# Relational graph layer on one core: the table stage's stores and order of work, and the queues of the sum stage, are rearranged

## The chip, the cores and the metric

The kernel runs on one core of a Trainium2 chip. The metric is the device time in microseconds (us) of one execution. Engines in the views: PE is the matrix engine, PEld its weight loads, DVE the vector engine, ACT the scalar engine, POOL the engine that issues the gathers, SP the engine that issues most other transfers. PEclk is the clock granted to PE as a share of its full 2.4 GHz.

## The reference

One layer on a graph of 12,500 nodes with 64 features and 200,000 edges, sorted by destination, each with one of 64 relations and a weight. `W` is made from a basis; then every edge brings its source's normed row, times weight, times its relation's 64×64 matrix, to its destination.

```
h = jnp.maximum(_layernorm(x, axis=-1), 0.0)
W = jnp.einsum('rb,bio->rio', comp, basis)
msg = h[src] * norm
s = segment_sum(msg, etype * N + dst, R * N).reshape(R, N, -1)
y = relu(jnp.einsum('rni,rio->no', s, W) + bias) + relu(h @ res_w.T + res_b)
out = x + (y - mean(y, 0)) * rsqrt(var(y, 0) + BN_EPS) * gamma + beta
```

Destinations crowd at low node numbers (drawn as a square), so a tile of 128 edges at the front of the list falls on very few nodes.

## The kernel before

**Two ways for an edge.** The list is cut into 1563 tiles of 128 edges. The first 528 (`HEAD`) are *heads*: the rows of x are gathered, normed, multiplied by a one-hot matrix of (node, relation) on PE and added up in an SBUF array `sacc`; at six chunk ends (after 215, 304, 373, 431, 482 and 528 heads, `HEAD_ENDS`) `sacc` is multiplied by `W` (32 matmuls, the "relations"), flushed into the accumulator `acc` and cleared. The other 1035 tiles read rows of a table: `z_table`, h times every relation's matrix, 800,000 rows of 64 numbers, 205 MB, which the kernel writes first.

**Table stage.** x lies in SBUF; DVE norms it in steps of 14 node tiles (`LNT`). For each of the 25 chunks of 512 nodes DVE duplicates the rows, PE transposes them (`transposed_x`), ACT takes the high part in bf16 with the relu (`first_part`, L684), DVE the remainder (the "split", L881), ACT casts that (`second_part`, L691). A chunk has four node tiles and each tile eight products (128 nodes by 8 relations × 64), each of three bf16 matmuls into one PSUM bank (L1238). ACT copies the banks into `zst` (L655); from node tile 24 (`DVE_FROM`) DVE takes the odd ones of three tiles in four (L983). There are four banks (`zps`), and seven once the metadata is done (chunk 15). `zst` has `NZS` = 4 buffers of `ZT` = 4 products, 1 MB each; SP stores each when full, 196 transfers with rows of 8 KB a partition. PE's order is written out in `jobs`: with `AHEAD` = 2, transposed x of chunk c, a step of metadata (`meta`), then all products of chunk c−2. DVE's order is: norm steps as due, duplicate, split, a metadata step (`take_meta`), its products of c−2. ACT: first part of c, second part of c−1, products of c−2. Statistics of the head (which base each chunk has, whether all fits) come in one piece with the metadata. Meanwhile POOL gathers the heads' rows of x (L590) and SP stores them by blocks of 8 to `head_rows` as `head_due` says.

**Tile stage.** One list `sums`, the same for PE, DVE and ACT, orders tiles and head items: between tiles 4 and about 800 the head items are dealt out evenly. POOL gathers one tile of table rows per instruction (L618) into a ring of 36 (`NY`); a slot is free when PE has used it. Four tiles are a unit: PE adds its products in PSUM (L1356), DVE adds the window into `acc` (`add_up`, L1088). Units have three banks in turn (`NAP`), and unit u's add comes at the end of unit u+2 (`LAG`). DVE makes the one-hots six tiles (L1105) and four heads (L1112) ahead. For heads, in blocks of eight: DVE's `centre` (L1135, after head 2 of the block before), ACT's squares (L749), DVE's `spread` (L1139, after 4), ACT's root, DVE's `factor` (after 5), ACT's two relus per head into `ab` (L762). PE multiplies head t (L1371) into one of `NHP` = 4 banks and first waits for the add of head t−4; DVE adds it to `sacc` (`add_head`, L1098) `HLAG` = 3 heads later, at a chunk end at once. At a chunk end PE runs the 32 relations (L1380), DVE at once waits for them and flushes (L1161), ACT then clears `sacc` in four instructions (L735), and the next adds wait for those. After the last unit the moments, the batch norm and the output follow.

Of the kernel before, what the change touches and what calls it, by code (L numbers as in the profile page):

```python
# [22 lines left out]
ZT = 4  # L23
NZS = 4
# [4 lines left out]
NAP = 3  # L29
LAG = 2  # L30
TILES_AHEAD, HEADS_AHEAD, HQ = 6, 4, 4
# [15 lines left out]
NHOH = 8  # L47
NHP = 4
HLAG = 3
REL_STEP = 1  # L50

# [27 lines left out]
def rgcn_kernel(nc, x, src, dst, etype, weight, basis, comp, bias, res_w, res_b, gamma, beta, out):  # L79
# [39 lines left out]
    METAS_AT = 4  # L119
    HKEYS_AT, ZROWS_AT = 2, 3  # L120
# [7 lines left out]
    epi_after = [unit_end[done_unit[k]] + (n + 1) * DONE_STEP  # L128
                 for k in range(len(DONE)) for n in range(done_from[k + 1] - done_from[k])]
    moments_at = [min(t + NOH + 1, NZT - 1) for t in epi_after]  # L130
# [55 lines left out]
    with ExitStack() as ctx:  # L186
# [54 lines left out]
        wcopy = zst[:, NZS - 1, :, :].rearrange("p t n -> p (t n)").rearrange("p (r f) -> p r f", f=F)  # L241
# [101 lines left out]
        AHEAD = 2  # L343
        jobs = [("comp",), ("resw",)] + [("w", n) for n in range(F // CLS)]
        for c in range(NCH + AHEAD):
            jobs += [("x", c)] if c < NCH else []
            jobs += [("z", r, t) for t in range((c - AHEAD) * 4, min((c - AHEAD + 1) * 4, NT)) if c >= AHEAD for r in range(NCLS)]
# [65 lines left out]
        def head_due(n):  # L413
            return max(0, min(NHB, int((62 + 3.05 * n - 34) / (1.28 * HB))))
# [213 lines left out]
        def _(e):  # L628
# [64 lines left out]
            def products(c):  # L693

                for n in range(c * BANK // P * NST, min((c + 1) * BANK // P, NT) * NST):
                    t, h = STORES[n]
                    rows = LAST if t == NT - 1 else P
                    if n == NZS - 1:
                        e.wait_ge(s_wd, 16)
# [9 lines left out]
            for kind, n in act_order:  # L709
# [12 lines left out]
            second_part(NCH - 1)  # L722
            products(NCH - 2)
            products(NCH - 1)
# [7 lines left out]
            with e.If(flag >= 1):  # L732
# [12 lines left out]
                for kind, n, *_ in sums:  # L745
# [27 lines left out]
                e.wait_ge(s_rel, NHK)  # L773
# [22 lines left out]
        def _(e):  # L796
# [89 lines left out]
            def stats_of_head():  # L886
# [6 lines left out]
                for k, (a, b) in enumerate(zip(chunk_from, HEAD_ENDS)):  # L893
                    e.tensor_reduce(over[:, k:k + 1], span_h[:, a:b], AX, ALU.max)
                    link(e.tensor_reduce(chunk_f[:, k:k + 1], base_h[:, a:b], AX, ALU.min))
                    link(e.tensor_scalar(base_h[:, a:b], base_h[:, a:b], chunk_f[:, k:k + 1], float(HALF), ALU.subtract, ALU.mult))
                    link(e.tensor_reduce(over[:, NHK + k:NHK + k + 1], base_h[:, a:b], AX, ALU.max))
                    e.tensor_scalar(over[:, k:k + 1], over[:, k:k + 1], float(HEAD_NODES[k] - 1), None, ALU.subtract)
# [294 lines left out]
        def _(e):  # L1193
# [97 lines left out]
            for c in range(NCH + AHEAD):  # L1291
                if c < NCH:
                    transposed_x(c)
# [143 lines left out]
```

## Time and profile before

| | us |
|---|---|
| median of 3 runs | 2539.49 |
| lowest, highest | 2535.84, 2551.64 |
| span of the profiled execution | 2559.4 |
| its table stage | 150 to 984 |
| its tile stage | 1047 to 2536 |

The profiled execution is 20 us longer than the median. The page tells each engine's share over the whole span; since the stages have different limits, the views by window are read after it. A window's row gives the busy time of PE, PEld, DVE, ACT and POOL with the number of instructions, then PEclk, the mean busy share of the DMA engines and their GB/s. A row of waits gives the engine, what it writes and its line, behind the arrow what released it, then us in total, times and the longest. In an order of time each row is start, duration, instruction and in brackets the idle time before it with its releaser. "remote" is a releaser that the profile can't name, "issue" is time in which the engine waited for nothing that shows.

### The profile page before, as it was taken

The page shows a single profiled execution, that of the slowest core. Times are in us where ns is not written, and L with a number is a line of the kernel's source. Part 1 is how long each engine was busy: PE and PEld are TensorE (multiplying, and loading weights), DVE is VectorE, ACT ScalarE, POOL GpSimd, SP SyncE. Part 2 cuts the span into 40 slices and gives each one's busy share as a digit, 9 for nine tenths or more (in the row PEclk, how much of TensorE's full clock was granted, in tenths as well). Part 3 has the DMA queues.
Part 4 walks back from the last instruction along what each step waited for, and adds up shares of the span by engine and source line. Part 5 has one row for each costly group of instructions (what it writes and reads, how often), then busy time and mean ns, then how long its engine had stood idle before and what let it go on. Part 6 is the DMA issues. An engine that isn't in the chain of part 4 may idle for free. (4 is left out here: it accounts for less than half of the span.)

```text
span 2559.4 us, 29252 instructions
## 1 busy us (share of the span) xinstructions
PE 1675.1 (65%) x6522; PEld 817.4 (32%) x6571; DVE 1040.2 (41%) x3394; ACT 1003.6 (39%) x2898; POOL 1474.2 (58%) x1565
## 2 busy tenths in 40 slices
PE   1267677867787767466666677768778787872223
PEld 1222222323233222244444434434434343331112
DVE  0442013335233211255555535636546363632324
ACT  0255543424343332655555526526436252610001
POOL 7265535554465553366666666666666666666664
PEclk9997878878798878555555575575565757575656
DMA  7066667767687765111111111111111111111112
GB/s 141 24 244 264 263 250 275 304 234 285 254 341 300 291 230 198 45 42 40 43 40 40 43 28 41 42 27 39 40 31 39 31 40 31 35 23 41 39 41 63
DMA packets 120893, 308.66 MB, mean 121 GB/s; under 512 B 49361, under 2 KB 49644, under 8 KB 95395
## 3 DMA queue, kind: packets, MB, share of 16 engines
q1 hardware_dynamic: 56622, 233.21, 23.4%
q0 software_dynamic: 49504, 50.79, 10.6%
q10 hardware_dynamic: 14588, 22.76, 3.2%
q8 instruction: 54, 0.88, 0.1%
q14 instruction: 125, 1.02, 0.1%
HBM read 80.28 MB, written 226.35 MB: 120 GB/s over the span
## 5 line engine op out<-in xcount | busy, mean ns | idle before, releaser
L618 POOL DMA_INDIRECT shared<-z_table,idx_all x1019 | 967.3, 949 | 605.8 <-issue 233.6
L590 POOL DMA_INDIRECT acc<-in_x,idx_all x520 | 493.9, 950 | 448.5 <-DMA head_rows<-acc 299.7
L1238 PE MATMUL zps<-wp,res 128*128 128x512 bf16 x1915 | 503.3, 414 | 188.8 <-issue 79.9
L655 ACT ACTIVATE zst<-zps 128x512 f32<-128x512 f32 x480 | 276.9, 599 | 365.3 <-PE zps L1238 223.1
L762 ACT ACTIVATE res<-res,hw 128x64 f32<-128x64 f32 x1056 | 357.5, 426 | 104.2 <-issue 53.8
L1371 PE MATMUL mps<-wp,res 128*128 128x160 f32 (+4 forms) x528 | 271.9, 620 | 158.7 <-issue 84.4
L1238 PEld LDWEIGHTS zps<-wp,res 128*128 128x128 bf16 x1956 | 190.1, 103 | 490.6 <-issue 164.5
L1105 DVE TENSOR_SCALAR shared<-iota,rel_all,wgt_all 128x36 f32<-128x36 f32 (+9 forms) x1035 | 307.9, 326 | 62.0 <-ACT res L729 61.5
L1356 PE MATMUL zps<-shared 128*64 128x36 f32 (+9 forms) x1354 | 208.3, 317 | 146.2 <-issue 72.7
L749 ACT ACTIVATE res<-res,hm 128x64 f32<-128x64 f32 x528 | 176.0, 334 | 224.9 <-issue 132.2
L1356 PEld LDWEIGHTS zps<-shared 128*64 128x64 f32 x1354 | 143.7, 197 | 351.6 <-issue 283.3
L983 DVE COPY zst<-zps 128x512 f32<-128x512 f32 (+1 forms) x172 | 117.6, 690 | 298.1 <-PE zps L1238 171.2
L1112 DVE TENSOR_SCALAR wp<-iota,rel_all,wgt_all 128x160 f32<-128x160 f32 (+4 forms) x528 | 211.8, 402 | 0.1
L1380 PE MATMUL zps<-zst,res 128*64 128x256 f32 x384 | 179.0, 608 | 28.6 <-issue 28.3
L1371 PEld LDWEIGHTS mps<-wp,res 128*128 128x128 f32 x528 | 131.7, 309 | 196.5 <-issue 112.0
L1356 PE MATMUL aps<-shared 128*64 128x36 f32 (+9 forms) x684 | 109.9, 316 | 86.7 <-issue 65.1
L1371 PE MATMUL zps<-wp,res 128*128 128x160 f32 (+4 forms) x264 | 136.8, 621 | 42.4 <-issue 25.2
L1371 PE MATMUL aps<-wp,res 128*128 128x160 f32 (+4 forms) x264 | 137.3, 622 | 40.5 <-issue 34.6
L1098 DVE TENSOR_TENSOR zst<-zst,mps 128x160 f32 (+4 forms) x264 | 95.8, 363 | 139.6 <-remote 67.7
L1356 PEld LDWEIGHTS aps<-shared 128*64 128x64 f32 x684 | 75.5, 196 | 195.1 <-issue 172.2
L735 ACT ACTIVATE zst<-ones 128x2048 f32<-128x2048 f32 x24 | 43.8, 1896 | 197.0 <-remote 197.0
L783 ACT ACTIVATE bmv<-bmv,eps 128x1 f32<-128x1 f32 x1 | 0.3, 294 | 295.5 <-DVE bmv L1175 295.5
(202 smaller groups left out, 1306.9 us busy)
## 6 DMA issues: line engine op xcount, KB each, us to landing
z_table<-zst SPq DMA_DIRECT2D x194, 1024.0 KB
wp<-z_table SPq DMA_DIRECT2D x1792, 0.2 KB
head_rows<-acc SPq DMA_DIRECT2D x66, 256.0 KB
res<-head_rows ACTq DMA_DIRECT2D x64, 256.0 KB
shared<-z_table,idx_all POOLq DMA_INDIRECT x1019
acc<-in_x,idx_all POOLq DMA_INDIRECT x520
wp<-z_table ACTq DMA_DIRECT2D x256, 0.2 KB
zst<-in_x ACTq DMA_DIRECT2D x12, 256.0 KB
```

The lines of the kernel that those rows point to most:

```text
L590: e.indirect_dma_start(out=ring[:, b % NRING, i, :], out_offset=None, in_=x, in_offset=bass.IndirectOffsetOnAxis(ap=idx_first[:, t:t + 1] ...
L618: e.indirect_dma_start(out=ys[:, q % NY, :], out_offset=None, in_=table[:, :], in_offset=bass.IndirectOffsetOnAxis(ap=idx_all[:, col:col + ...
L655: e.activation(to, frm, ACT.Copy).then_inc(s_ez, 1)
L749: last = e.activation(hsq[:, i, :], hs[:, n % 2, i, :], ACT.Square, bias=hm[:, n % 2, 0, i:i + 1], accum_out=hm[:, n % 2, 1, i:i + 1])
L762: last = e.activation(ab[:, t % NABS, a, :], hs[:, n % 2, i, :], ACT.Relu, scale=hw[:, n % 2, 0, i, a:a + 1], bias=hw[:, n % 2, 1, i, a:a ...
L983: e.tensor_copy(zst[0:rows, n % NZS, i, :], bank_of(job)[0:rows, :]).then_inc(s_dz, 1)
L1105: e.tensor_scalar(oh[:, t % NOH, 0:w], iota[:, 0:w], rel_all[:, col:col + 1], wgt_all[:, col:col + 1], ALU.is_equal, ALU.mult).then_inc(s_ ...
L1112: e.tensor_scalar(hoh[:, t % NHOH, 0:w], iota[:, 0:w], rel_all[:, t:t + 1], wgt_all[:, t:t + 1], ALU.is_equal, ALU.mult).then_inc(s_hoh, 1)
L1238: last = e.matmul(to, lhsT=stationary(px, pw), rhs=moving(px, pw), start=(a == 0), stop=(a == 2))
L1356: e.matmul(unit_psum(u)[h:h + F, 0:w], lhsT=rows, rhs=oh[:, t % NOH, 0:w], start=(k < 2), stop=(k >= size - 2)).then_inc(s_agg, 1)
L1371: e.matmul(head_psum(t)[:, 0:w], lhsT=ab[:, t % NABS, :, :].rearrange("p a f -> p (a f)"), rhs=hoh[:, t % NHOH, 0:w], start=True, stop=Tru ...
L1380: last = e.matmul(zps[0:F, NZB - 1, 0:SUM_NODES], lhsT=wf[:, q, :], rhs=by_relation[:, q, :], start=(q == 0), stop=(q == HALF - 1))
```

## The change

The stores: `ZT` 4 → 2 and `NZS` 4 → 8, so 392 transfers of 512 KB with rows of 4 KB; the buffers together keep their size. The order of the table stage: PE now does the eight products of a chunk's first tile, then transposes x of the next chunk, then the products of its other three; ACT likewise puts the first part between products of tile 0 and 1, the second part between 1 and 2; DVE does the split and a metadata step of chunk c ahead of its products of c−1. Statistics of the head are done one chunk at a time in six chunks, the decision on the fast path after them. The tile stage: `NAP` and `LAG` are gone; four units share one bank in turns of two, and their adds come together, six tiles after the group's end; three last units stay alone. One-hots are made ten tiles and six heads ahead (eleven head buffers). Heads have five banks. `centre` comes after head 0 of a block, `factor` after head 6. At a chunk end four "drain" items add the waiting heads, `sacc` is cleared in quarters, each when eight relations are done, and the flush comes eight items later.

```
-ZT = 4
-NZS = 4
+ZT = 2
+NZS = 8
-NAP = 3
-LAG = 2
-TILES_AHEAD, HEADS_AHEAD, HQ = 6, 4, 4
+UG = 4
+ADD_LATE = 6
+TILES_AHEAD, HEADS_AHEAD, HQ = 10, 6, 4
-NHOH = 8
-NHP = 4
+NHOH = 11
+NHP = 5
+FLUSH_LATE = 8
+    added_at = [t + ADD_LATE for t in group_end[:LONE]] + [t + 2 for t in group_end[LONE:]]
-        if b + 1 < NHB and k in (2, 4, 5):
-            head_items.append(({2: "centre", 4: "spread", 5: "factor"}[k], b + 1))
+        if b + 1 < NHB and k in (0, 4, 6):
+            head_items.append(({0: "centre", 4: "spread", 6: "factor"}[k], b + 1))
-            head_items += [("relations", n, r) for r in range(0, HALF, REL_STEP)] + [("flush", n)]
+            head_items += [("drain", n)] * (HLAG + 1)
+            head_items += [("relations", n, r) for r in range(0, HALF, REL_STEP)] + [("clear", n)]
+    for n in reversed(range(NHK)):
+        late = FLUSH_LATE if n + 1 < NHK else 0
+        head_items.insert(head_items.index(("clear", n)) + 1 + late, ("flush", n))
...
-            return max(0, min(NHB, int((62 + 3.05 * n - 34) / (1.28 * HB))))
+            return max(0, min(NHB, int((62 + 3.05 * n / 2 - 34) / (1.28 * HB))))
...
-            return (mps[:, 0, :], mps[:, 1, :], zps[:, 0, :], aps[:, 1, :])[t % NHP]
+            return (mps[:, 0, :], mps[:, 1, :], zps[:, 0, :], aps[:, 1, :], zps[:, 2, :])[t % NHP]
-            return (aps[:, 0, :], zps[:, 1, :], zps[:, 2, :])[u % NAP]
+            if u >= LONE:
+                return (aps[:, 0, :], zps[:, 2, :], zps[:, 1, :])[u - LONE]
+            return (aps[:, 0, u % UG * WIN:(u % UG + 1) * WIN], zps[:, 1, u % UG * WIN:(u % UG + 1) * WIN])[u // UG % 2]
...
-                    first_part(n)
                     c = n - X0
                     if c >= 1:
-                        second_part(c - 1)
-                    if c >= 2:
-                        products(c - 2)
+                        products(tiles_of(c - 1)[0:1])
+                    first_part(n)
+                    if c == 0:
+                        second_part(c)
+                    elif c >= 1:
+                        products(tiles_of(c - 1)[1:2])
+                        second_part(c)
+                        products(tiles_of(c - 1)[2:])
...
-                    elif kind == "flush" and n + 1 < NHK:
-                        e.wait_ge(s_rel, n + 1)
-                        for a in range(0, SUM_NODES * HALF, 2048):
-                            clear(sacc[:, a:a + 2048]).then_inc(s_flush, 1)
+                    elif kind == "clear" and n + 1 < NHK:
+                        for q in range(NSC):
+                            e.wait_ge(s_rel, NSC * n + q + 1)
+                            part = sacc.rearrange("p (n r) -> p n r", r=HALF)[:, :, q * HALF // NSC:(q + 1) * HALF // NSC]
+                            e.activation(part, ones[:, 0:1].unsqueeze(2).broadcast_to([P, SUM_NODES, HALF // NSC]),
+                                         ACT.Copy, scale=0.0).then_inc(s_flush, 1)
...
+                    if STATS_AT <= c < STATS_AT + NHK:
+                        stats_of_chunk(c - STATS_AT)
+                    if c == STATS_AT + NHK:
+                        fast_path_or_not()
+                    if c >= 1:
+                        products(c - 1)
...
-                        if k == size - 1 and u >= LAG:
-                            add_up(u - LAG)
+                        while added[0] < len(units) and added_at[added[0]] == t:
+                            add_up(added[0])
...
-                        while len(heads) > (0 if t + 1 in HEAD_ENDS else HLAG):
+                        while len(heads) > HLAG:
                             add_head(heads.pop(0))
+                    elif kind == "drain" and heads:
+                        add_head(heads.pop(0))
...
-                        if k == 0 and u >= NAP:
-                            e.wait_ge(s_acc, u - NAP + 1 + NCLEAR)
+                        if k == 0 and u % UG == 0 and u >= 2 * UG:
+                            e.wait_ge(s_acc, u - UG + NCLEAR)
+                        if u == len(units) - 1 and k == 0:
+                            e.wait_ge(s_acc, LONE + NCLEAR)
```

## Rows read from the trace of the kernel before

**Rows 1.** The page: span, busy share of each engine, two DMA queues.

```profile
span 2559.4 us, 29252 instructions
PE 1675.1 (65%) x6522; PEld 817.4 (32%) x6571; DVE 1040.2 (41%) x3394; ACT 1003.6 (39%) x2898; POOL 1474.2 (58%) x1565
...
q1 hardware_dynamic: 56622, 233.21, 23.4%
...
q10 hardware_dynamic: 14588, 22.76, 3.2%
```

**Rows 2.** Windows: from:to length, busy of PE PEld DVE ACT POOL, clock, DMA, GB/s.

```profile
150.00:984.00 834.00, 613.49 (x2462) 244.63 (x2510) 245.47 (x444) 351.63 (x613) 425.77 (x449) 0.84 0.73 281
741.00:762.00 21.00, 20.47 (x95) 9.23 (x96) 8.94 (x15) 11.09 (x21) 11.38 (x13) 1.00 0.93 367
600.00:622.00 22.00, 9.85 (x32) 3.64 (x33) 12.41 (x48) 7.47 (x13) 9.48 (x11) 0.69 0.43 155
1073.30:1464.50 391.20, 264.83 (x963) 169.61 (x963) 225.61 (x939) 223.83 (x883) 246.38 (x260) 0.50 0.19 41
1464.50:1500.70 36.20, 31.69 (x127) 13.88 (x127) 9.72 (x43) 5.19 (x16) 23.30 (x26) 0.82 0.15 30
2167.50:2259.40 91.90, 70.97 (x202) 33.53 (x200) 55.20 (x191) 49.08 (x169) 58.22 (x61) 0.55 0.15 32
```

**Rows 3.** The gathers of L618: two windows of that line, one in order.

```profile
990.00:2530.00 1540.00, 966.48 (x1019) 0.58 0.17 37
2252.00:2530.00 278.00, 179.05 (x191) 0.60 0.17 35
...
1502.85 0.94 POOL L618 DMA_INDIRECT shared<-z_table,idx_all  x1 [0.30 <-issue]
```

**Rows 4.** Waits from 1047 to 2291, heads' adds, spread and `ab`.

```profile
DVE zst L1098 <- remote: 129.2, 48, 5.6
DVE zst L1098 <- PE mps L1371: 88.9, 58, 3.9
PEld mps L1371 <- ACT res L762: 65.0, 32, 23.1
DVE hm L1139 <- ACT res L749: 46.6, 17, 15.9
```

**Rows 5.** Chunk ends: idle before L1161, a clear, who waited for L735.

```profile
  remote: 67.5, 6
...
1510.01 7.31 ACT L735 ACTIVATE zst<-ones 128x2048 f32<-128x2048 f32 x4 [40.32 <-remote]
...
  DVE zst L1098: 16.3, 4
```

**Rows 6.** Waits from 2291 to 2530, the tail without heads.

```profile
DVE acc L1088 <- remote: 147.7, 27, 11.7
PEld zps L1356 <- DVE acc L1088: 51.4, 8, 11.6
```

**Rows 7.** Table stage in order of time, then its waits from 150 to 984.

```profile
133.72 0.63 ACT L691 ACTIVATE res<-shared 64x512 bf16<-64x512 f32 x1
...
140.54 0.60 ACT L684 ACTIVATE res<-zps 128x512 bf16<-128x512 f32 x1 [1.76 <-PE zps L1195]
...
141.82 0.60 ACT L655 ACTIVATE zst<-zps 128x512 f32<-128x512 f32 x1
...
392.32 1.46 PE L1238 MATMUL zps<-wp,res 128*128 128x512 bf16 x3 [3.01 <-DVE res L881]
...
393.24 1.07 DVE L970 CAST idx_all<-mps 128x520 int32<-128x520 f32 x1
...
PEld zps L1238 <- DVE res L881: 18.7, 8, 4.6
...
PE zps L1238 <- DVE res L881: 14.3, 6, 3.7
```

**Rows 8.** DMA issues from 0 to 1000: KB each, us to landing.

```profile
w_full<-zst SPq DMA_DIRECT2D x1, 1024.0 KB, 3.9
```

More of the change, by code:

```diff
@@ L119, in rgcn_kernel @@
     METAS_AT = 4
+    STATS_AT = METAS_AT + len(METAS) + 1
+    assert METAS[-1] == "zstats" and STATS_AT + NHK < NCH
     HKEYS_AT, ZROWS_AT = 2, 3
@@ L342, in rgcn_kernel, with tiles_of @@
         s_cols, s_low = sem("s_cols"), sem("s_low")
[L343 to L347, printed above, removed]
+        CT = BANK // P
+        def tiles_of(c):
+            return range(c * CT, min((c + 1) * CT, NT))
+        jobs = [("comp",), ("resw",)] + [("w", n) for n in range(F // CLS)] + [("x", 0)]
+        for c in range(NCH):
+            for t in tiles_of(c):
+                jobs += [("z", r, t) for r in range(NCLS)]
+                jobs += [("x", c + 1)] if t == c * CT and c + 1 < NCH else []
         jobs += [("r", n) for n in range(NEPI)]
@@ L691, in second_part, with products @@
                 e.activation(xp[F:P, c, 0, 0:w], rem[F:P, n % 2, 0:w], ACT.Copy).then_inc(s_p2, 1)
-            def products(c):
-                for n in range(c * BANK // P * NST, min((c + 1) * BANK // P, NT) * NST):
+            def products(tiles):
+                for n in range(tiles[0] * NST, (tiles[-1] + 1) * NST):
                     t, h = STORES[n]
                     rows = LAST if t == NT - 1 else P
-                    if n == NZS - 1:
+                    if n == NZS - HALF * F // (ZT * BANK):
                         e.wait_ge(s_wd, 16)
@@ L973, in products @@
             def products(c):
-                for n in range(c * BANK // P * NST, min((c + 1) * BANK // P, NT) * NST):
+                for n in range(c * CT * NST, min((c + 1) * CT, NT) * NST):
                     t, h = STORES[n]
@@ L1003, in _ @@
                         rows_of_table(c - ZROWS_AT, (GA, GB)[c - ZROWS_AT])
[L1004 to L1008 removed]
+                    if METAS_AT < c <= METAS_AT + len(METAS):
+                        take_meta(c - METAS_AT - 1)
+                    if STATS_AT <= c < STATS_AT + NHK:
[4 more added lines that the diff above has]
+                        products(c - 1)
             products(NCH - 1)
@@ L1162, in _ @@
                         e.wait_ge(s_hout, t + 1)
-                for u in range(len(units) - LAG, len(units)):
-                    add_up(u)
+                while added[0] < len(units):
+                    add_up(added[0])
                 e.wait_ge(s_acc, len(units) + NCLEAR)
@@ L1289, in meta @@
                     last.then_inc(s_mt, 1)
-            for c in range(NCH + AHEAD):
-                if c < NCH:
-                    transposed_x(c)
-                if 0 <= c - AHEAD - METAS_AT < len(METAS):
-                    meta(c - AHEAD - METAS_AT)
-                if c >= AHEAD:
-                    for t in range((c - AHEAD) * 4, min((c - AHEAD + 1) * 4, NT)):
-                        for r in range(NCLS):
-                            product(r, t)
+            transposed_x(0)
+            for c in range(NCH):
+                if METAS_AT <= c < METAS_AT + len(METAS):
+                    meta(c - METAS_AT)
+                for t in tiles_of(c):
+                    for r in range(NCLS):
+                        product(r, t)
+                    if t == c * CT and c + 1 < NCH:
+                        transposed_x(c + 1)
             for n in range(NEPI):
```

54 lines of the change are left out of this document (26 added, 28 removed).

## The prediction

> **What bounds the kernel now.** I read the page first, then the windows by stage, then the waits of each stage, then the order of time around single waits. The page [rows 1] shows no engine at its peak: PE is busy 65% of the 2559.4 us and POOL 58%. The share must be read by stage [rows 2].
>
> *Table stage, 150 to 984 (834 us).* PE is busy 613.49 of it at a clock of 0.84, the DMA engines 0.73. The stretch 741 to 762 shows what it can do: 20.47 of 21 us busy, clock 1.00, DMA 0.93. So PE and the stores are both near a bound when nothing interrupts, and what can be won are interruptions. 834 − 613 = 221 us of PE idling is the most.
>
> *Tile stage, about 1047 to 2536.* POOL issues 1019 gathers from 990 to 2530 [rows 3]. When nothing holds it, one takes 0.94 us plus 0.30 us ahead of it, 1.25 us with rounding: 1019 × 1.25 = 1274 of 1540 us. The other 266 us it waited until a row of its ring of 36 came free, that is, for PE. In that stage POOL's rate is a floor, and no change of PE, DVE or ACT can win more than 266 us. Three places hold it up:
> - Windows with heads. From 1073.3 to 1464.5 there are 215 heads in 391.2 us, 1.82 us each, PE busy 264.83 at a clock of 0.50, the lower of its two levels (1.2 of 2.4 GHz) [rows 2]. DVE's adds wait 129.2 us on "remote" and 88.9 us on PE, DVE's spread waits 46.6 us for ACT's squares, and PE 65.0 us for ACT's `ab` [rows 4]. PE may run head t only once head t−4 is added: a ring of four banks. A round of product, evacuating add and the wait back takes 4 × 1.82 = 7.3 us.
> - Chunk ends. DVE waits 67.5 us in six flushes, then ACT clears `sacc` in 7.31 us and DVE's next adds wait 16.3 us in four places [rows 5]. While it waits, one-hots and adds of tiles stand behind it in its queue, and PE's window units behind those.
> - The tail without heads. DVE's adds of units wait 147.7 us in 27 places, up to 11.7 us, and PE waits 51.4 us in 8 for those adds [rows 6]. They work in lockstep: unit u needs the add of u−3, which DVE reaches only after another unit. POOL issues 191 gathers in 278 us there, 191 × 1.25 = 239: 39 us lost.
>
> **The change part by part.** The sum is made against the profile's span of 2559.4 us.
>
> *1. Start of the products.* Before, ACT evacuates the first product at 141.82, behind x's third bank at 140.54, which waits for DVE's norm; the second part for chunk 0 is cast at 133.72 [rows 7]. Afterwards product 0 needs x's chunk 0 alone. 141.82 − 134.4 = 7.4 at most; one transposition and three matmuls come first: −6. Bounds 0 and −7.
>
> *2. Order of x and products.* Before, transposed x stands ahead of a chunk's products in PE's queue, and DVE's norm steps ahead of the split of chunk data. At 392.32 PE had waited 3.01 us for it; over the stage 18.7 + 14.3 = 33 us in 14 places [rows 7]. Now the eight products of tile 0 lie ahead of it: at 21/32 = 0.66 us a product, 5.2 us of cover, more than 4.6, the longest. Without that cover the 33 us come back. I take −20, since other waits take over some; bounds 0 and −33.
>
> *3. The metadata step and the split now come right before DVE's first odd product*, with four banks. PE runs at most four products beyond it. Eleven chunks have such a step; the cast alone takes 1.07 us [rows 7]. Nothing shows what it costs in this place: between 0 and the 3.01 us of the same kind of wait. Half: 11 × 1.4 = +15.
>
> *4. Statistics of the head spread over six chunks.* In 600 to 622 PE is busy 9.85 of 22 us, DMA 0.43 [rows 2]. By the stage's mean (613.49/834 = 0.74) it would be 16.2, at full speed 22: 6.4 to 12 us lost. The instructions stay, in six pieces of under 1.5 us, covered by the banks: −8.
>
> *5. Stores of 512 KB.* 196 transfers and their waits are added on SP, whose queue has only stores and head rows in this stage. Rows of 4 KB replace rows of 8 KB. q1, by bytes nearly all rows of 8 KB, costs 23.4% of 2559.4 for 233.21 MB, 2.57 us a MB of all engines; q10, of short rows, 3.2% for 22.76 MB, 3.6 us a MB [rows 1]. I take a tenth of that difference (rows of 4 KB lie next to those of 8 KB): 205 MB × 0.1 = 20 us of DMA time, hidden under the DMA's idle 27% (7% at full speed). In exchange a buffer comes free after two products, not four. I take 0; bounds −10 (buffers earlier) and +20 (nothing hidden).
>
> Table stage: −6 − 20 + 15 − 8 + 0 = −19.
>
> *6. Chunk ends: flush eight items late, four quarter clears, drains.* The flush no longer waits for a matmul chain just begun; between relations and flush lie heads and tiles. ACT clears quarters while PE still does the next eight relations, so three of four clears (5.5 of 7.31 us) are covered. 67.5 + 16.3 = 84 us are the most [rows 5]; the last flush has no such delay, and a strided clear may take longer than 1.9 us: −75. Bounds −84 and −20 (if PE, busy 31.69 of 36.2 us there [rows 2], only shifts the wait into its own time).
>
> *7. Windows with heads: fifth head bank, one-hots six heads and ten tiles ahead, centre two items earlier, factor one later.* The loop of 7.3 us holds five heads: 1.46 us a head by this bound. But a head window holds tiles too, which POOL feeds at 1.25 us. Head windows last about 2291 − 1047 − 218 (six ends) = 1026 us; POOL's loss there is 266 less the tail's 39, so at most −227. Against it: PE waits for ACT's `ab`, 65.0 us, and DVE for ACT's squares, 46.6 [rows 4]; these don't go with the bank. And PE's busy time is 0.68 of the window at half clock. I take about a quarter: −60. Bounds 0 and −227.
>
> *8. Tail: adds of four units together, six tiles after the group's end.* PE may be two groups ahead. POOL can give back 39 us [rows 3]; the last three units stay alone, and six tiles of lateness come at the end only (they are not late for those): −15. Bounds 0 and −39.
>
> Total: −19 − 75 − 60 − 15 = −169, so 2390 us in the profile. The profile of before is 20 us longer than the median of its runs (2559.4 against 2539.49), so **2370 us**, −6.7%.
>
> A rule of the Trainium skill bears on part 5. The row: one store of 1 MB alone took 3.9 us to land [rows 8], against 2.57 us of work per MB [rows 1], so 1.3 us doesn't scale with its size. The Trainium skill, "DMA: Bandwidth & Descriptors", section "Bandwidth", says to batch transfers to at least 1 MiB for three quarters of peak; by it the change goes the wrong way.
>
> **The rivals.**
>
> *A. PE itself is the bound of the head windows* (chance 0.14). At clock 0.50 it is busy 70.97 of 91.9 us in a late window [rows 2], 77%, with matmuls that come back late. Then the fifth bank gives nothing, and the late flush only half (−38). 2559 − 19 − 38 − 5 − 20 = 2477, about 2480. Against: DVE's and ACT's waits in [rows 4] have other releasers too.
>
> *B. Nothing that can be measured* (0.10). The time saved at ends is lost in windows that POOL's ring had evened out: 2540.
>
> *C. Slower: x between tile 0 and tile 1 makes DVE late for the odd products of tile 1* (0.08). With four banks PE stops in each chunk, and its clock falls: a chunk that ran 21 us at clock 1.00 is about 35 us long on average (834/24.5 is 34). If 10 us are lost in each of the 19 chunks where DVE takes products, +190; with parts 6 to 8 as forecast (−150) that is 2540 + 40 = about 2580. It decides from 8 us a chunk.
>
> *D. The finer stores are serial in what doesn't scale* (0.03): 1.3 us × 196 more transfers = +255, with −169: 2540 + 86 = 2625. Against it: at full speed 1 MB leaves each 2.6 us, shorter than the 3.9 it takes alone, so transfers overlap. This is also what the rule of the page just named would give.
>
> The order of adds (factor one item later) can also hurt: `ab` comes up to 1.82 us later in each of 66 blocks, 120 us at most, which would undo parts 7 and half of 6, and end near rival A.
>
> **How the numbers follow.** Forecast 0.65, A 0.14, B 0.10, C 0.08, D 0.03. The forecast's own range is from 2290 (−80 more in part 7) to 2450 (parts 6 and 7 at their weak ends by half). With A inside, 2290 to 2505 leaves out B, C and D (0.21) and almost nothing below. A measurement of this kernel tells about 1% from no change. Faster by over 1% are the forecast and A, 0.79; within 1% B, 0.10; slower by over 1% C and D, 0.11.
>
> **What would show it.** Table stage: the waits of PE on DVE's `res` gone at chunk boundaries (part 2), none over 4 us before products after a metadata step (3), no hole of 8 us at the head's statistics (4), DMA share not above 0.80 with stores of 512 KB (5); its length 815 us. Chunk ends: the flush waits under 15 us in total, adds of heads don't wait for the clear. Head windows: under 1.7 us a head. Tail: adds of units wait under 100 us, 191 gathers in under 265 us. The prediction is wrong if the head windows stay at 1.82 us, or if PE idles on DVE's products of each tile 1.

## The result: 1.3% faster on the chip of the profiles, where 6.7% was forecast, and 0.3% on another

| | us |
|---|---|
| before, median of 10 runs | 2538.8 (2525.2 to 2551.6) |
| changed, median of 10 runs | 2510.4 (2484.0 to 2531.2) |
| ratio, 95% interval | 0.987 (0.984 to 0.991) |
| span of the changed kernel's profiled execution | 2482.0 |

The forecast was 2370 us, 2290 to 2505. The measured gain is 28 us, not 169. The ratio leaves out two runs of the changed kernel (2521.6 and 2531.2 us), as they are over 1.5% above its fastest; the medians of all ten have a ratio of 0.989. The changed kernel's profile is of its fastest execution, 28 us below the median; that of before was 20 us above its own. So the 77 us between the two spans overstate the change by about 48.

The page of the changed kernel: engines, the DMA queue of the stores, and the gathers' group (busy, mean ns, idle ahead of it and its main releaser).

```profile
span 2482.0 us, 30002 instructions
...
PE 1657.6 (67%) x6571; PEld 823.8 (33%) x6571; DVE 1049.9 (42%) x3394; ACT 999.7 (40%) x2898; POOL 1473.2 (59%) x1565
...
q1 hardware_dynamic: 84754, 233.22, 24.5%
...
L636 POOL DMA_INDIRECT shared<-z_table,idx_all x1019 | 966.5, 949 | 571.3 <-issue 242.4
```

q1 now has 84,754 packets for the same bytes: 608 us of 16 engines (24.5% of 2482.0), against 599 (23.4% of 2559.4) in [rows 1]. So rows of 4 KB cost 1.5% more DMA time; the prediction had put 20 us, it is 9. (On the other chip, below, it is 606 us in e1 against 601 in e4, which has rows of 8 KB: 5 us.)

Windows of the changed kernel: table stage, first window with heads, first chunk end, tail. Columns as in [rows 2].

```profile
150.00:932.00 782.00, 599.26 (x2505) 241.56 (x2506) 251.49 (x471) 346.34 (x614) 424.71 (x448) 0.88 0.80 297
1018.20:1390.90 372.70, 251.85 (x943) 165.47 (x943) 223.35 (x922) 223.27 (x882) 237.01 (x250) 0.50 0.17 42
1390.90:1433.90 43.00, 33.23 (x136) 15.77 (x135) 14.13 (x59) 11.14 (x19) 27.88 (x30) 0.71 0.13 30
2219.60:2462.90 243.30, 87.24 (x444) 46.64 (x440) 76.58 (x265) 0.00 (x0) 154.78 (x164) 0.55 0.15 36
```

Against [rows 2]: the table stage ends 51 us earlier in this profile (last store issued at 932 instead of 983). The 215 heads of the first window take 372.7 instead of 391.2 us, but 257 tiles lie among them instead of 267, because the list of head items has grown; the first chunk end takes 43.0 us with 34 tiles instead of 36.2 with 30. A tile costs 1.45 us instead of 1.47 in the window, 1.26 instead of 1.21 at the end. Over the whole stage, from the first tile's product to the last, the two profiles have 1491.6 and 1470.0 us. The work was moved between windows; hardly any of it became cheaper.

The gathers in the same profile, all of them and the tail's, then those of before in the first window and the tail:

```profile
938.00:2455.00 1517.00, 965.60 (x1019) 0.57 0.15 38
2219.60:2455.00 235.40, 153.85 (x164) 0.55 0.15 37
```

```profile
1073.30:1464.50 391.20, 246.38 (x260) 0.50 0.19 41
2291.20:2530.00 238.80, 154.07 (x164) 0.56 0.18 37
```

All engines in that tail of before:

```profile
2291.20:2530.00 238.80, 56.27 (x382) 29.66 (x380) 63.80 (x235) 0.00 (x0) 154.07 (x164) 0.56 0.18 37
```

This is what the prediction read past. A gather takes 1.50 us in before's first head window, where PE is busy 68% of the time, and 1.46 us in its tail, where PE is busy 24% and ACT not at all. In the changed kernel it is 1.49 and 1.44. A loss that is nearly equal over such different work is hardly the work's; the experiments test that. The prediction took it for three different waits of PE and DVE and priced each.

What such a wait looks like in the tail of before, in order of time (rows of one unit's matmuls, the add that needs them, and PE's next matmul):

```profile
2405.57 0.49 PE L1356 MATMUL zps<-shared 128*64 128x78 f32 x8
...
2414.94 0.24 DVE L1088 TENSOR_TENSOR acc<-acc,aps 128x78 f32 x1 [9.90 <-remote]
...
2415.23 0.52 PE L1356 MATMUL aps<-shared 128*64 128x78 f32 x2 [9.17 <-issue]
```

For nine microseconds PE, DVE and ACT all stand still, while POOL issues five gathers and then waits too. PE's wait is named "issue": nothing that the profile shows holds it. Between the first tile and the last, PE and its weight loads stand still for over 1 us in 117 places in before, 419 us in all, and in 141 places, 393 us, in the changed kernel; 16 of the first and 4 of the second are over 8 us. The change cut the long holes into shorter ones and left their sum nearly as it was. (On the other chip, below, e1 has 50 places, 113 us.)

### The profile page after: what moved, and what is told of

Its sections match the earlier page's. It is cut to its first block and busy times, and to the rows that moved or that the text cites. A ratio compares the mean times of both kernels' runs of the same rounds, so it can differ in the third digit from the quotient of the medians.

```text
span 2482.0 us, 30002 instructions
## 1 busy us (share of the span) xinstructions
PE 1657.6 (67%) x6571; PEld 823.8 (33%) x6571; DVE 1049.9 (42%) x3394; ACT 999.7 (40%) x2898; POOL 1473.2 (59%) x1565
## 3 DMA queue, kind: packets, MB, share of 16 engines
q1 hardware_dynamic: 84754, 233.22, 24.5%
## 5 line engine op out<-in xcount | busy, mean ns | idle before, releaser
L673 ACT ACTIVATE zst<-zps 128x512 f32<-128x512 f32 (+1 forms) x482 | 275.7, 601 | 346.7 <-PE zps L1270 221.7
L1405 PE MATMUL mps<-wp,res 128*128 128x160 f32 (+4 forms) x424 | 212.8, 607 | 131.9 <-ACT res L782 75.5
L1405 PE MATMUL zps<-wp,res 128*128 128x160 f32 (+4 forms) x422 | 215.5, 612 | 103.7 <-issue 42.4
L1390 PE MATMUL aps<-shared 128*64 128x36 f32 (+9 forms) x1024 | 167.9, 314 | 83.3 <-issue 73.7
L1390 PE MATMUL zps<-shared 128*64 128x48 f32 (+9 forms) x1014 | 159.7, 317 | 56.1 <-issue 51.4
L1390 PEld LDWEIGHTS aps<-shared 128*64 128x64 f32 x1024 | 114.1, 195 | 231.9 <-issue 231.5
L1390 PEld LDWEIGHTS zps<-shared 128*64 128x64 f32 x1014 | 111.2, 197 | 205.7 <-issue 204.6
L1010 DVE COPY zst<-zps 128x512 f32<-128x512 f32 x171 | 115.4, 687 | 151.3 <-PE zps L1270 96.2
L1405 PEld LDWEIGHTS zps<-wp,res 128*128 128x128 f32 x422 | 105.2, 307 | 128.6 <-issue 55.4
L1405 PE MATMUL aps<-wp,res 128*128 128x160 f32 (+4 forms) x210 | 107.3, 611 | 51.2 <-issue 26.3
L901 DVE SCALAR_TENSOR_TENSOR shared<-zps,res 128x512 f32<-128x512 f32 (+1 forms) x21 | 14.3, 679 | 283.3 <-issue 201.2
```

What stands on the lines that cost most here:

```text
L673: e.activation(to, frm, ACT.Copy).then_inc(s_ez, 1)
L1010: e.tensor_copy(zst[0:rows, n % NZS, i, :], bank_of(job)[0:rows, :]).then_inc(s_dz, 1)
L1390: e.matmul(unit_psum(u)[h:h + F, 0:w], lhsT=rows, rhs=oh[:, t % NOH, 0:w], start=(k < 2), stop=(k >= size - 2)).then_inc(s_agg, 1)
L1405: e.matmul(head_psum(t)[:, 0:w], lhsT=ab[:, t % NABS, :, :].rearrange("p a f -> p (a f)"), rhs=hoh[:, t % NHOH, 0:w], start=True, stop=Tru ...
```

## The experiments

Three theories stand in the expectations. T: the gain lies in the table stage, and the sum stage (the tile stage, after the table) is bound by things that the change leaves alone. S: the sum stage gained what the prediction says, and it is given back elsewhere. G, formed after the second set of runs: on some chips PE runs slowly while POOL issues gathers, whatever PE does. "Slow chip" and "fast chip" are short names for where the kernel before takes about 2550 and 1977 us.

### On another chip, the parts apart

The first four runs fell on a chip that runs the kernel before in 1977 us instead of 2539. All ratios here are to runs of before on the same chip.

```
e1: the changed kernel, unchanged
e2: before + the hunks of the table stage (jobs, products, splits, statistics, ZT, NZS, head_due)
e3: before + the hunks of the sum stage (UG, ADD_LATE, NHP, NHOH, *_AHEAD, items, clear, drain)
e4: changed, but
-ZT = 2
-NZS = 8
+ZT = 4
+NZS = 4
```

> The changed kernel once more, for its profile. The one profile at hand has a span of 2482.0 us, where its ten runs have a median of 2510. Theory T (the gain lies in the table stage; the sum stage is bound by PE's own time and by POOL's rate and moved little): 2500 to 2520 us, the last table store near 940 us, from the first tile to the last 1470 to 1495 us. Theory S (the sum stage really gained as the prediction said, some 100 us, and is given back at another place): from the first tile to the last under 1430 us in this profile.

> The kernel before with only the table stage's part of the change: order of x and products, spread statistics, stores of 512 KB. Theory T: nearly the whole gain, 2500 to 2515 us (ratio 0.985 to 0.99), last store near 940 us instead of 983. Theory S: 2520 us (the 19 us of the sum), and the rest from the sum stage. If the short stores cost what the rival D says: above 2540.

> The kernel before with only the sum stage's part of the change: late flush, clear in quarters, five head banks, one-hots further ahead, four units to a bank. Theory T: within 0.6% of before, 2525 to 2545 us. Theory S: 2390 to 2450 us (the 150 us of the sum). If the parts work against each other here: above 2550.

> The changed kernel with stores of 1 MB in four buffers again, all else as changed. The prediction put the finer stores at 0 (bounds -10 to +20 us): then 2500 to 2520 us, like the changed kernel. If the earlier free buffer is what shortened the table stage: 2530 or more, the last store back near 975 us. If 512 KB stores cost time: under 2495 us.

| | median us | ratio | 95% |
|---|---|---|---|
| before | 1977.4 | | |
| e1 changed | 1970.7 | 0.997 | 0.996 to 0.998 |
| e2 table part | 1972.6 | 0.997 | 0.997 to 0.998 |
| e3 sum part | 1974.7 | 0.999 | 0.998 to 1.000 |
| e4 stores of 1 MB | 1970.0 | 0.996 | 0.995 to 0.998 |

Neither theory foresaw the 1977 us. The changed kernel on this chip (page, then windows of the table stage, the first head window and the tail, and the gathers' own window):

```profile
span 1967.2 us, 30002 instructions
...
PE 1600.7 (81%) x6571; PEld 808.6 (41%) x6571; DVE 1062.8 (54%) x3394; ACT 996.1 (51%) x2898; POOL 1475.7 (75%) x1565
...
POOL 7777777777777777777777777777777777777775
...
L608 POOL DMA_INDIRECT acc<-in_x,idx_all x520 | 496.7, 955 | 158.5 <-issue 158.2
```

```profile
71.10:658.90 587.80, 544.54 (x2537) 235.65 (x2537) 254.69 (x471) 345.55 (x617) 445.19 (x468) 1.00 1.02 397
711.20:1016.10 304.90, 249.37 (x944) 165.69 (x943) 219.35 (x926) 222.90 (x882) 230.87 (x243) 0.50 0.24 51
1709.90:1945.70 235.80, 110.49 (x437) 56.00 (x436) 83.85 (x259) 0.00 (x0) 178.20 (x189) 0.55 0.20 41
```

```profile
670.00:1946.00 1276.00, 965.43 (x1019) 0.62 0.21 45
```

The first head window of e2, which has the sum stage of before:

```profile
710.50:1014.50 304.00, 266.23 (x965) 174.52 (x965) 223.01 (x942) 227.96 (x897) 230.07 (x243) 0.50 0.23 51
```

POOL's row of tenths is 7 from end to end: it issues 528 + 1019 = 1547 gathers at 1.25 us, 1934 us, with no wait but the 0.30 us ahead of each. 1276 us for 1019 gathers is the floor of 1274 that [rows 3] gave, to 2 us. The table stage is at 397 GB/s, DMA 1.02, with POOL's gathers of heads ending 11 us behind its last store. So there both stages are at floors that no part of the change touches; what it gains are 5 to 8 us. Finer stores neither help nor hurt: 1970.7 against 1970.0 (part 5 of the prediction right here, rival D wrong; e4 was not run on a slow chip). The rule that the Trainium skill states in "DMA: Bandwidth & Descriptors", section "Bandwidth", batches of 1 MiB or more for three quarters of peak, doesn't show in this stream of stores, where many are in flight: 512 KB a transfer give the same time as 1 MB, at 397 GB/s with the gathers' traffic counted in.

e2 also settles what the waits of the sum stage are worth. With before's own order of that stage, this chip takes 304.0 us for the window of 391.2 us in [rows 2], at the same clock of 0.50, with 243 gathers at 1.25 us. The waits that part 6 priced stand there unchanged. The idle time ahead of e2's flush (67.5 us in [rows 5]):

```profile
  PE zps L1397: 67.3, 6
```

Its adds wait 16.6 us for the clear in four places (16.3 in [rows 5]). Yet its sum stage, from the first tile to the last, takes 1265 us, and e1's and e3's, where hardly any of these waits are left, take 1263 and 1261: under POOL's floor they cost next to nothing.

### Half of the gathers, fewer and more matmuls (a slow chip: before 2566.8 us)

```
e5, e6 (before, changed):
                 for q, t in enumerate(pool_tiles):
+                    if q >= NY and q % 2:
+                        continue
...
-                            e.wait_ge(s_y[q % NY], 16 * (q // NY + 1))
+                            e.wait_ge(s_y[q % NY], 16 * (1 if q % 2 else q // NY + 1))
e7 (changed):
-                for a, (px, pw) in enumerate(((0, 0), (0, 1), (1, 2))):
+                for a, (px, pw) in enumerate(((0, 0), (1, 2))):
...
e8 (changed), in product:
+                for k in range(0, BANK, BANK // 2):
+                    last = three_parts(b[:, k:k + BANK // 2], ..., [:, k:k + BANK // 2])
```

> The kernel before without every second gather of table rows after the first 36: PE takes the old rows of that slot, the rest is as it was. POOL's time for the gathers falls from 1274 to about 660 us. Where POOL's rate is the floor of the sum stage (as in the runs of the last call, 1.25 us a gather throughout), the time falls until PE, DVE and ACT bind: some 1.0 to 1.15 us a tile, 1750 to 1850 us on that chip. Where PE binds (as in the profile shown of before, 2559 us), nothing changes: over 2480 us.

> The same on the changed kernel. This pair tells what the sum stage's part of the change is worth with POOL's floor taken away. If the parts do what the prediction says, and POOL's floor alone hid it: 60 to 150 us below the same edit of before. If the head windows and chunk ends are PE's own time: within 20 us of it.

> The changed kernel with the products of two matmuls instead of three (the second part is left out): 800 matmuls and 800 loads of weights fewer, PE's time in the table stage down by a third. If the table stage is bound by its stores (DMA share 0.97 in the last call's profiles): less than 15 us gained. If by PE: the stage falls by 100 us or more. If what a slow chip adds goes by the number of PE's instructions (some 570 us over 13,800 of them, 0.041 us each): 65 us less there by that alone.

> The changed kernel with each matmul of a product cut in two of 256 columns: the same columns, 2400 matmuls and 2400 loads more. On a chip like that of the last call (1970 us): less than 30 us more. On a chip like the one of the profiles shown (2500 us), if PE's instructions come late there: 4800 x 0.041 = some 200 us more. If the slow chip is slow for another reason: less than 60 us more there too.

| | median us | ratio | 95% |
|---|---|---|---|
| e5 before, half gathers | 2169.4 | 0.847 | 0.841 to 0.852 |
| e6 changed, half gathers | 2174.3 | 0.847 | 0.840 to 0.853 |
| e7 two matmuls a product | 2490.7 | 0.971 | 0.965 to 0.978 |
| e8 matmuls cut in two | 2645.1 | 1.033 | 1.026 to 1.041 |

e5 was to leave the time over 2480 us if PE bound the sum stage by its own work. It fell by 397 us, with every matmul in place. (The 1750 to 1850 us of its other case were meant for a fast chip; e16 below has 1748.5 there.) First head window and tail of e5, then the first head window of e6:

```profile
1079.80:1361.80 282.00, 255.95 (x963) 167.87 (x963) 215.99 (x935) 222.98 (x882) 126.29 (x133) 0.50 0.18 42
2006.20:2145.70 139.50, 58.23 (x440) 31.96 (x438) 70.33 (x264) 0.00 (x0) 73.92 (x78) 0.61 0.19 43
```

```profile
1088.50:1392.60 304.10, 249.32 (x943) 165.62 (x943) 216.80 (x926) 222.88 (x882) 120.67 (x128) 0.50 0.16 39
```

The window of 391.2 us in [rows 2] takes 282.0 here, PE busy 91% at the same clock of 0.50 and the same 963 matmuls. POOL's floor for its 260 gathers is 325 us, and PE beside half of the gathers can do it in 282; that the two together take 391 and not 325 is the slow chip's doing, since e2 above runs at POOL's floor with the same order. So in the profile of before PE was held up by the gathers, not by banks, adds or flushes. And the pair e5, e6 says what the whole change is worth with half of them out of the way: nothing (0.847 both); from the first tile to the last e6 takes 1103 us, e5 1092. In the first window the changed order is even slower, 1.41 us a head against 1.31, and faster later (1.44 and 1.46 against 1.58 in the fourth and fifth).

e7 and e8 bear on whether PE's instructions are slow on such chips by themselves. The control on the same chip is e6, whose table stage is the changed kernel's: its last store is issued at 1000 us. A third less PE work in the products makes that 944 us: 57 us for 800 matmuls, not the 100 or more of a stage that PE binds. Twice the instructions for the same columns makes it 1066, 66 us more for 2400 matmuls and as many loads. By the medians e7 is 43 us and e8 some 110 us from the changed kernel, if that is at 0.987 of before here too: e7 between the 15 and the 65 of its cases, e8 between the 60 and the 200. Neither has a run on the fast chip, so they don't tell the causes apart.

### Without the gathers of heads, held gathers, and the parts again (a slow chip: before 2560.8 us)

```
e9 (changed):
             for t in range(HEAD):
+                if t >= NRING * HB:
+                    continue
...
-                e.wait_ge(s_hg[b % NRING], 16 * HB * (b // NRING + 1))
+                e.wait_ge(s_hg[b % NRING], 16 * HB)
e10 (changed):
             for t in range(HEAD):
+                if t == FIRST:
+                    e.wait_ge(s_pz, 2 + F // CLS)
e11, e12: the kernels of e2 and e3
```

> The changed kernel without POOL's gathers of x rows after the first 64 of 528; the stores of head rows and everything else stay. Theory G (on the slow chip PE runs slowly while POOL issues gathers, whatever the data): there the products run as on the other chip, 21 to 25 us a chunk, so the table stage is some 200 us shorter and the whole under 2330 us; the start to 95 us stays slow, since the first 64 gathers stay. If PE is slow there by itself: over 2450 us. On the other chip: the table stage shorter by the end of POOL's gathers only, about 20 to 60 us.

> The changed kernel, but POOL's ninth gather of x rows waits until PE has made W (all work stays). On the slow chip PE makes W at one instruction in 0.70 us until 95 us, while 64 gathers run; theory G: W is done by 45 us instead, the first product 50 to 70 us earlier, and the end by as much, if POOL's gathers of heads catch up: 2440 to 2470 us. If the slow start has another cause: unchanged, 2500 to 2520. On the other chip POOL is the bound from start to end, and the held gathers come on top: 30 to 60 us slower.

> The kernel before with only the table stage's part, once more, for a chip of the slow kind. There the changed kernel gains 1.3%. Theory T (the gain is the table stage's): ratio 0.982 to 0.992. If the gain is the sum stage's: 0.995 to 1.005. On a chip of the other kind: 0.997 again.

> The kernel before with only the sum stage's part, once more. Theory T: ratio 0.994 to 1.003 on either kind of chip, and no fewer microseconds a tile than 1.44 where the chip is slow. If the sum stage's part is worth what half of the prediction says (75 us): 0.97.

| | median us | ratio | 95% |
|---|---|---|---|
| e9 no gathers of heads after 64 | 2258.6 | 0.883 | 0.879 to 0.886 |
| e10 gathers held until W is made | 2541.4 | 0.993 | 0.990 to 0.995 |
| e11 table part | 2555.1 | 0.998 | 0.996 to 1.001 |
| e12 sum part | 2558.7 | 1.000 | 0.997 to 1.003 |

e9 against e11, windows of the table stage from the first products to the last store, on the same chip:

```profile
141.60:688.70 547.10, 528.81 (x2490) 245.11 (x2538) 252.60 (x471) 355.71 (x617) 0.00 (x0) 1.00 1.01 399
```

```profile
138.00:969.00 831.00, 616.62 (x2481) 247.79 (x2529) 253.40 (x474) 352.00 (x620) 434.76 (x458) 0.85 0.77 282
```

Without POOL's gathers this "slow" chip does the stage in 547 us with PE busy 97% at full clock and 399 GB/s, as fast as the fast chip does it with fills in their place (554 us at 395 GB/s in e14 below). With them PE's busy time is 88 us longer, at a clock of 0.85, and its idle time 196 us longer. In the sum stage of e9, where the gathers are back, it is slow again: 1486.9 us from the first tile to the last. Eight us at a time, with the products that ACT and DVE copied out of PSUM (all 776 of full width are in each trace) sorted by the gathers that POOL issued in the same stretch; means over eight placings of the stretches, which differ by up to 0.8 each way where there are gathers and by up to 2.0 where there are none:

```
gathers in 8 us      0      1-3    4-5    6-7
before              9.9     9.1    7.6    6.0   products
changed             9.2     9.3    8.3    6.6
e11                 9.2     9.1    7.9    6.0
e9, no gathers     11.3      -      -      -
e1, fast chip        -       -      -    10.5
```

The start shows it bare. PE makes `W` by many small matmuls; POOL's first 64 gathers run from 3.8 to 85.4 us. In order of time, the changed kernel in its first profile, then e1 on the fast chip, then e10 on a slow one:

```profile
83.83 0.26 PE L1254 MATMUL zps<-compT,res 64*64 64x64 f32 x1 [2.52 <-issue]
86.63 0.26 PE L1254 MATMUL zps<-compT,res 64*64 64x64 f32 x1 [2.54 <-issue]
...
92.23 0.26 PE L1254 MATMUL zps<-compT,res 64*64 64x64 f32 x1 [0.44 <-issue]
92.93 0.26 PE L1254 MATMUL zps<-compT,res 64*64 64x64 f32 x1 [0.44 <-issue]
93.63 0.26 PE L1254 MATMUL zps<-compT,res 64*64 64x64 f32 x1 [0.44 <-issue]
```

```profile
18.02 14.31 PE L1254 MATMUL zps<-compT,res 64*64 64x64 f32 x192 [6.19 <-DMA res<-in_L_gnn_basis]
```

```profile
17.88 14.29 PE L1256 MATMUL zps<-compT,res 64*64 64x64 f32 x192 [5.98 <-DMA res<-in_L_gnn_basis]
```

All 256 records of these matmuls are in each trace. From 22.6 to 95.0 us the changed kernel's first profile has 32 of them, 2.3 us each, most often 2.8 us apart and never less than 0.70; behind 95.0 us the last 181 come at full pace. ACT takes the first two banks of `W` at 71.2 and 95.2 us there, at 20.7 and 23.0 on the fast chip and at 20.5 and 22.9 in e10. With the gathers held PE makes 192 matmuls in 14.29 us, as on the fast chip, and the first product starts at 63.1 instead of 134.4 us. But the 50 to 70 us that e10 was to gain didn't arrive: its first chunk of 32 products is copied out from 64.2 to 173.0 us, beside the gathers that were held (e1: 64.5 to 88.2), and its last store is issued at 970.9 as in e11 (969.3). The gathers were moved, and their price with them. Theory G holds in its mechanism; its forecast for e10 was wrong.

The parts alone give 6 and 2 us here. That refutes theory T for the table part (0.982 to 0.992 expected, 0.998 measured) and theory S for the sum part (0.97 for half of the forecast, 1.000 measured, 0.997 to 1.003). In all the profiles of such chips with all gathers of rows of the table, in either order, the sum stage takes nearly the same: before 1491.6, changed 1470.0, e7 1499, e8 1488, e9 1487, e10 1491, e11 1493, e12 1489 us. That is 1019 gathers at 1.44 to 1.47.

### What of a gather, and the later factor (a fast chip: before 1977.2, then 1975.8 us)

```
e14, e18 (changed), for heads from 64 on:
+                    e.memset(ring[:, b % NRING, :, :], 1.0)   (twice, each waited for)
e15 (changed), for heads from 64 on:
+                    e.dma_start(ring[:, b % NRING, i, :], x[128 rows in order])
e16 (e6):
-        if b + 1 < NHB and k in (0, 4, 6):
+        if b + 1 < NHB and k in (0, 4, 5):
```

> The changed kernel as it is, hoped for on a slow chip, beside the parts measured there alone (table part 0.998, sum part 1.000). Theory T+ (the parts add up): ratio 0.995 to 1.000. If they only work together: 0.987 again as in the first measurement. On a fast chip: 0.997.

> The changed kernel with POOL's gathers of x rows after the first 64 replaced by two fills of 128 by 512 each, about as long: POOL is as busy, but makes and starts no transfers (the heads' rows are then ones). On a slow chip: if it is POOL's being busy that slows PE, about 2520 to 2560 us; if it is the gathers' transfers or the making of them, 2260 us as without them, chunks of 21 to 23 us.

> The changed kernel with those gathers replaced by POOL-issued plain transfers of 128 consecutive rows of x, the same 32 KB. On a slow chip: if any transfer that POOL makes slows PE, about 2500 us as before; if only the indirect ones do, under 2330 us.

> As the changed kernel with half of the table gathers, with factor after head 5 of a block again instead of 6. There the first head window took 1.42 us a head, where the kernel before took 1.32 and PE was busy 0.91 instead of 0.82. If the later factor is what makes the relus late: the window back to 1.33 us a head, some 15 to 20 us less over all head windows. If not: unchanged.

> The changed kernel as it is, once more, for a slow chip. If the parts add up (0.998 and 1.000 measured alone on such a chip): ratio 0.994 to 1.001. If the first measurement's 0.987 holds on each slow chip: 0.984 to 0.991. On a fast chip: 0.996 a third time.

> The changed kernel with fills instead of POOL's gathers of x rows after the first 64, for a slow chip: POOL busy without transfers. If POOL's being busy slows PE there: 2500 us or more. If the gathers' transfers or the making of them do: 2220 to 2280 us, as without any gathers (2259). On a fast chip: 1938 again.

All six fell on fast chips. The changed kernel: 1969.8 us, 0.996 (0.995 to 0.998), and 1971.3 us, 0.998 (0.996 to 0.999). Fills instead of gathers: 1937.7 and 1936.8 us, 0.980 both; the table stage's last store goes from 659 to 625 us, so on a fast chip the gathers of heads cost the stores 34 us, at the DMA's limit. Plain transfers: 1980.7 us, 1.002, last store at 670, no cheaper than indirect ones. What these two were made for, telling POOL's being busy from its transfers on a slow chip, stays open.

e16 took 1748.5 us. Its first head window:

```profile
712.10:997.90 285.80, 248.76 (x946) 165.46 (x945) 216.29 (x927) 223.26 (x883) 126.66 (x135) 0.50 0.18 42
```

285.8 us for 215 heads, 1.33 us each as its expectation said, against 1.41 in e6. PE waits for ACT's `ab` 45.1 + 10.2 + 5.7 = 61 us there against 45.8 + 17.9 + 10.2 = 74 in e6. But e6 ran on a slow chip and e16 on a fast one, and no run on the fast chip has half of the gathers and the late factor. e1's 1.42 there is no control: it is POOL's floor (243 gathers at 1.25 us are 304), and e2, with the factor early, takes 304.0 us too. All six head windows together are 44 us shorter in e16 than in e6, where 15 to 20 were expected, so the chip has a share in it. That the later factor costs some 18 us in the first window, a risk that the prediction had named behind its rivals, fits but isn't shown. While all gathers are there, e1 and e2 show no cost of it.

## Why the prediction was wrong, point by point

**The base of all of it.** "The other 266 us it waited until a row of its ring came free, that is, for PE" was right by the waits and wrong as a gain. PE was late because POOL was gathering; with PE late POOL waited; the two settle at 1.44 to 1.50 us a gather. The step that failed is the sum of parts 6, 7 and 8: it gave 150 of these 266 us back to the order of work, taking each wait for its nearest releaser's own cost. The runs show in its place: the whole sum part is worth 2 us on a slow chip (e12, 1.000, from 0.997 to 1.003) and 3 on a fast one (e3, 0.999); before's order runs at POOL's floor where gathers don't slow PE (e2); and on a slow chip the time goes with the gathers (e5, 397 us for half of them).

**Part 1** came as said: first product at 134.4 instead of 140.7 us. **Part 2** hardly came. Its 33 us count the same stops twice: all six waits of PE in [rows 7] lie inside waits of PEld, which stand for the same stop, so 18.7 us in 8 places were the most. In the changed kernel:

```profile
PEld zps L1270 <- DVE res L903: 11.4, 6, 5.3
...
PEld mps L1270 <- DVE res L903: 4.4, 1, 4.4
...
PE zps L1270 <- DVE res L903: 7.3, 5, 4.4
...
PE mps L1270 <- DVE res L903: 3.9, 1, 3.9
```

PEld's two rows are 15.8 us in 7 places, up to 5.3: −3 instead of −20 for part 2 alone, and the signs "gone" (part 2) and "none over 4 us" (part 3) both failed. Parts 2 and 3 together were forecast at −5 and are at −3; that the sum is near is luck. **Part 4**: the hole at the statistics is gone: behind 400 us no 7 us pass without a product copied out, in this profile and in e11's, where before and e12 have 14.3 and 15.6 us near 595; no run took it alone. **Part 5**: 0, right on the fast chip. The table stage as a whole: −19 forecast; the last store comes 51 us earlier in the first profile of the changed kernel, but 17 earlier in e11's than in e12's on one chip, and 10 later in e6's than in e5's on another; the medians of e11 give 6 us. The profile of before and the first one after lie on either side of their medians. So the −19 is neither confirmed nor refuted by single profiles, and 6 us is the best measure of the stage.

**Part 6, −75.** The waits went as described: DVE's flush waits 67.5 us in [rows 5], now

```profile
  remote: 8.3, 1
  issue: 1.1, 2
```

and the adds wait 7.5 us for the clear instead of 16.3. None of the 75 us arrived. In [rows 2] the chunk end of 36.2 us held 30 tiles, 1.21 us a tile, already faster than the windows between, while POOL issued 26 gathers. And e2 keeps these very waits and loses next to nothing by them. The term was put at 75 and should have been 0: it counted waits on DVE instead of tiles.

**Part 7, −60.** The fifth bank could take away only what PE waited for the adds, and the prediction read DVE's side of it. PE's side in before, the whole stage:

```profile
PE zps L1371 <- DVE zst L1098: 16.0, 16, 3.1
...
PE mps L1371 <- DVE zst L1098: 15.6, 16, 2.6
...
PE aps L1371 <- DVE zst L1098: 4.8, 7, 2.7
```

36 us in 39 places, so −60 was more than the bank could give. "The loop of 7.3 us" was no loop: four heads take 4 × 1.82 us whatever sets the 1.82. Measured: 0, for parts 6 to 8 together (e12, 1.000). The first head window is at 1.73 us a head, between the prediction's signs of right (under 1.70) and wrong (1.82), but with fewer tiles among the heads.

**Part 8, −15**: the tail has 243.3 us instead of 247.7 between the same marks in the profiles, and 251.1 in e12 against 247.5 in e11, which has before's order, on one chip: 0.

**The rivals.** A (2480, chance 0.14) lies 30 us from 2510; it had the head windows right as gaining nothing, but for PE's own work, which e5 refutes. B's 2540 is as near. C and D didn't come. Within the range's logic the failure was one assumption under all cases: that the 266 us belonged to the order of work.

**Open.** The changed kernel has 0.987 on the first chip, while its parts have 0.998 and 1.000 on another of the slow kind; whether that is the chip, or the parts together, no run tells, so the 28 us have no shown cause. That POOL's gathers slow PE is shown by e5, e9 and e10; by which way is not. Instruction supply is one guess, but the packets that carry instructions take no longer there: 0.37 and 1.02 us on the two queues in before, 0.39 and 1.12 in e1. Whether POOL's issuing or its transfers do it was left untested (e14, e15 and e18 all fell on fast chips). And that the chip makes the difference, and not something that changes with time on one chip, isn't shown: no chip is known to have been measured at two times.

## What to carry to other kernels

Before pricing waits one by one, divide the stage's time by its count of the one thing that every window has (here gathers): a rate that is nearly the same at 68% and at 24% PE busy points to that thing. For a ring between two engines, take the consumer's waits on the freed slot, not the evacuator's waits for data, as the most that another slot can give. Don't add PE's and PEld's waits for one releaser: they are mostly one stop. And a profile from one chip tells of that chip: the kernel before takes 1977 us on one and 2539 to 2567 on others.

## What was not expected of the hardware

- Two kinds of chip, as far as these runs tell: the kernel before has medians of 1975.8 to 1977.4 us in three sets of runs, and 2538.8, 2560.8 and 2566.8 us in three others; a gather of POOL that waits for nothing takes 0.94 + 0.30 us on both.
- On the slow kind 6.0 to 6.6 products are copied out in 8 us beside 6 or 7 gathers and 9.2 to 9.9 beside none, against 10.5 on the fast kind. At the start PE makes 32 small matmuls in 72.4 us there, until 10 us after the first 64 gathers are out; with the gathers held, or on the fast kind, it makes 192 in 14.3 us.
- Without 464 of the gathers of heads the changed kernel is 302 us below before on a slow chip, some 0.6 us for each gather left out; with fills in their place it is 32 us below the changed kernel on a fast one.
- One profile can lie 28 us below the median of its kernel's runs and another 20 us above: together more than the change.
